# One-hots of 128 lanes and a masked copy of the gathered rows, in a GNN kernel's collecting stages

## The chip, the cores and the metric

The kernel runs on one core of a Trainium2 chip. The metric is the device time of one execution in microseconds; the time before is the median of three runs.

## The reference

There are 12500 nodes with 16 features, and 400000 edges (src, dst), sorted by dst. Two layers, each followed by a residual and a layernorm over the 16 features:

```python
# layer 0
F_s = householder(reflection(xs, xd)); F_d = householder(reflection(xd, xs))
L_sd = -einsum('eki,ekj->eij', F_s, F_d)
msg_s = coef[:, None] * einsum('eij,ej->ei', L_sd, xd)
msg_d = coef[:, None] * einsum('eji,ej->ei', L_sd, xs)
out = relu(x - zeros.at[src].add(msg_s) - zeros.at[dst].add(msg_d))
# layer 1, twice (W1, b1), (W2, b2): gcn_conv and tanh
agg = segment_sum((h @ W)[row] * norm[:, None], col, num_segments=N)
```

What matters here is the sum over the edges of a node: the scatter to dst in layer 0, and the segment sums of the two graph convolutions. Below they are collect 0, 1 and 2.

## The kernel before

Nodes are kept in blocks of 128 (NB = 98 of them), and two blocks make a wide block of 256 nodes (NW = 49). The kernel sorts the edges twice into wide blocks, by src and by dst, in chunks of CH = 8 edges a partition. Each stage that needs a node's row for an edge, or adds an edge's row to a node, does it with one-hot matrices on TensorE: a tile is 128 edges (one a partition), its one-hot says which of the block's nodes the edge belongs to. Values are split into three bf16 pieces, so a row has 3 * D = 48 columns.

Around the change there are these stages, in the profiled execution's time. The message stage (2416 to 5083 us) computes the messages in src order, adds those for src, and writes those for dst to DRAM rows of CH * RW values (msg_rows); RW = 3 * D + 2 leaves room for the key of the edge's dst node behind the 48 values. Collect 0 (5083 to 5803) gathers these rows in dst order and adds them to the nodes. Then, twice, a stage that expands the nodes' values in src order and writes them to val_rows (5847 to 6340, 6993 to 7488), and a stage that collects them in dst order (6340 to 6962, 7488 to 8105).

A collect has G2 = 293 groups of 16 tiles, one after the other, all in loops written out for each engine, four groups a pass (q = 0 to 3):

- GpSimd (gather_rows, the gather at L601) issues one indirect DMA a group into got[q]. It waits until TensorE is done with the group four before, and in collect 0 for that group's keys too.
- ScalarE in collect 0 (copy_keys, L913 and L914) copies the keys from the rows to dst_key, in pairs; collects 1 and 2 use them again. In all three (far_hots2) it makes the one-hots of the last 2 tiles by Abs and Relu (L895, L901, L906).
- VectorE (collect, turn) waits in collect 0 for the keys, then adds the sums of the group three before (add_group: L1812 loads an address, L1679 adds 96 columns from PSUM to acc), then makes the one-hots of the other 14 tiles (lanes, L1670) in lane_hot2[q]. A one-hot is 256 wide, both halves of a wide block.
- TensorE (sums, L1159) waits for rows, one-hots and a free PSUM bank, and runs for each tile one matmul for the lower and one for the upper 128 nodes, each with 48 columns.

acc holds 48 columns for each block of 128 nodes, lower then upper. Behind a collect VectorE reduces the three pieces to agg (L1850, L1884) and goes on with the node-wise part. src_rel, dst_rel and later dst_key share the memory of rel_all. The names lane_hotb and wide_hotb in the profile are the buffers 0, 1 and 2, 3 of lane_hot2; wide_hotb is also used by the expanding stages.

## Time and profile before

| | us |
|---|---|
| median of 3 runs (lowest to highest) | 7817.33 (7814.12 to 7823.55) |
| profiled execution, first to last instruction | 8142.6 |
| message stage, in the profile | 2667 |
| collect 0, 1, 2 | 720, 622, 617 |
| the two expanding stages | 493, 495 |

The profiled execution stands for its kernel with one time only, its span; nothing is given of what lies around that, and it is 325 us longer than the median. Times in a timeline count from the span's start. In its rows a number in brackets is the idle time of the engine before the instruction, and what ended it; "issue" means that the profile shows nothing that the engine waited for. An instruction's next one can start up to 0.1 us before the shown end. Rows of TensorE merge a run of matmuls (x32).

### The profile page before, as it was taken

The numbers are of one execution on the slowest core, as the hardware profiler recorded it, in microseconds if no ns is written. First come the engines' busy times: TensorE is split into PE (matmuls) and PEld (weight loads), VectorE is DVE, ScalarE is ACT, GpSimd is POOL, SyncE is SP. The second block draws the span as 40 slices with busy tenths as digits, with TensorE's granted clock in tenths as the row PEclk, the third lists the DMA queues.
The fourth block names the chain that finished last, engine by engine and source line by source line (L and its number), as shares of the span: only waits on it lengthen the run. The fifth ranks groups of instructions, "written<-read, shape, count | busy, mean of one in ns | idle before, by whom it ended". The sixth has DMA issues, their size and how long they took to land.

```text
span 8142.6 us, 284433 instructions
## 1 busy us (share of the span) xinstructions
PE 5258.0 (65%) x105060; PEld 4635.4 (57%) x105060; DVE 7026.3 (86%) x9716; ACT 5313.1 (65%) x12774; POOL 3318.7 (41%) x2217
## 2 busy tenths in 40 slices
PE   3431000677759899999999987566466666566665
PEld 2321000566647777777777776555455566555665
DVE  6559993555559999999999999999899999999999
ACT  4534130222228888888888887888666788567886
POOL 3340006666643333333333332555200788101886
PEclk8655555888878777778777777555566555566555
DMA  3000000888863333333333332333499433697333
GB/s 45 12 20 5 0 13 13 307 292 299 294 225 99 105 105 103 104 103 104 104 105 105 105 104 84 94 85 85 112 295 296 123 94 94 199 295 237 94 94 78
DMA packets 510651, 1043.86 MB, mean 128 GB/s; under 512 B 125636, under 2 KB 316420, under 8 KB 497508
## 3 DMA queue, kind: packets, MB, share of 16 engines
q1 hardware_dynamic: 376804, 761.05, 27.3%
q0 software_dynamic: 113856, 281.66, 13.7%
q10 hardware_dynamic: 19904, 0.13, 0.2%
q8 instruction: 38, 0.62, 0.0%
q14 instruction: 49, 0.40, 0.0%
HBM read 756.40 MB, written 286.18 MB: 128 GB/s over the span
## 4 chain that ended last, share of the span: by engine, by line
DVE 32%; issue 25%; PE 21%; ACT 7%; DVEq 6%; another core or an unknown queue 3%; ACTq 2%; POOL 2%; DMA 2%; POOLq 0%; SPq 0%
PE ps L1159 11%; PE ps L1054 6%; DVE wide_hotb L1871 3%; PE ps L1193 3%; DVE keys L1387 3%; DVEq L1812 3%; ACT apartb L901 3%; DVEq L1674 2%; DVE whole L1763 2%; DVE mirr L1767 2%; DVE acc L1679 2%; DVE low L1770 2%; DVE prod L1731 2%; DVE keys L1386 2%
## 5 line engine op out<-in xcount | busy, mean ns | idle before, releaser
L601 POOL DMA_INDIRECT xs_buf<-xd_rows,src_idx x488 | 871.2, 1785 | 1809.0 <-DVE mirr L1767 1668.3
L601 POOL DMA_INDIRECT got<-val_rows,dst_idx x586 | 1045.4, 1784 | 1259.6 <-DMA val_rows<-val_out 1075.3
L1871 DVE TENSOR_SCALAR wide_hotb<-sw_inb,slot_id 128x2048 bf16<-128x2048 bf16 x976 | 922.1, 1015 | 53.0 <-PE ps L1193 52.9
L1133 PEld LDWEIGHTS ps<-w2c,hid 128*128 128x128 f32 x7808 | 942.8, 197 | 13.4
L1084 PEld LDWEIGHTS ps<-wide_tab,wide_hot 128*128 128x128 bf16 x23424 | 634.1, 102 | 521.7 <-DVE wide_hot L1664 493.7
L1133 PE MATMUL ps<-w2c,hid 128*128 128x32 f32 x7808 | 919.8, 278 | 0.0
L1670 DVE TENSOR_TENSOR lane_hotb<-rel_all,iota_b 128x3584 bf16<-128x3584 bf16 x441 | 892.8, 2025 | 11.5 <-ACT rel_all L914 7.0
L1670 DVE TENSOR_TENSOR wide_hotb<-rel_all,iota_b 128x3584 bf16<-128x3584 bf16 x438 | 886.8, 2025 | 0.2 <-ACT rel_all L914 0.2
L1159 PE MATMUL ps<-got,lane_hotb 128*128 128x48 bf16 x14112 | 642.2, 215 | 369.3 <-DVE acc L1679 187.4
L1193 PE MATMUL ps<-wide_tabb,wide_hotb 128*128 128x48 bf16 x15616 | 626.3, 205 | 369.2 <-DVE wide_hotb L1871 253.4
L1054 PE MATMUL ps<-row_tab,dst_hot 128*128 128x64 bf16 x15744 | 669.9, 204 | 273.2 <-issue 238.3
L1159 PE MATMUL ps<-got,wide_hotb 128*128 128x48 bf16 x14016 | 635.2, 214 | 321.5 <-DVE acc L1679 187.3
L1159 PEld LDWEIGHTS ps<-got,lane_hotb 128*128 128x128 bf16 x14112 | 585.6, 117 | 425.9 <-DVE acc L1679 224.4
L901 ACT ACTIVATE apartb<-iota_b,rel_negb 128x256 bf16<-128x256 bf16 x1758 | 797.6, 500 | 40.1 <-ACT rel_negb L895 0.3
L1193 PEld LDWEIGHTS ps<-wide_tabb,wide_hotb 128*128 128x128 bf16 x15616 | 580.7, 111 | 414.9 <-ACT val_out L952 341.3
L1084 PE MATMUL ps<-wide_tab,wide_hot 128*128 128x32 bf16 x23424 | 659.8, 185 | 226.0 <-DVE wide_hot L1664 222.6
L1159 PEld LDWEIGHTS ps<-got,wide_hotb 128*128 128x128 bf16 x14016 | 582.4, 117 | 374.2 <-issue 186.5
L1054 PEld LDWEIGHTS ps<-row_tab,dst_hot 128*128 128x128 bf16 x15744 | 586.8, 105 | 356.7 <-issue 333.6
L601 POOL DMA_INDIRECT src_key<-chunk_keys,src_idx x488 | 609.7, 1249 | 338.6 <-ACT xd_out L758 197.1
L758 ACT ACTIVATE xd_out<-ps 128x512 f32<-128x512 f32 (+1 forms) x384 | 199.8, 534 | 618.2 <-remote 402.9
L1617 DVE COPY_PREDICATED xd_out<-row_upper,ps 128x512 f32<-128x512 uint8 (+1 forms) x384 | 217.4, 636 | 415.2 <-ACT xd_out L758 403.4
L601 POOL DMA_INDIRECT got<-msg_rows,dst_idx x293 | 408.2, 1393 | 353.6 <-ACT rel_all L914 269.5
(392 smaller groups left out, 11976.3 us busy)
## 6 DMA issues: line engine op xcount, KB each, us to landing
dw_in<-dst_wide SPq DMA_DIRECT2D x96, 1312.0 KB
xd_rows<-xd_out SPq DMA_DIRECT2D x128, 984.0 KB
sw_in<-src_wide SPq DMA_DIRECT2D x244, 512.0 KB, 4.3
sw_inb<-src_wide SPq DMA_DIRECT2D x244, 512.0 KB, 5.1
val_rows<-val_out SPq DMA_DIRECT2D x488, 192.0 KB, 4.1
sw_inb<-src_byte SPq DMA_DIRECT2D x244, 256.0 KB
msg_rows<-msg_out SPq DMA_DIRECT2D x244, 200.0 KB, 2.4
dw_in<-dst_byte SPq DMA_DIRECT2D x32, 656.0 KB
```

Of the source, the lines that this page charges most:

```text
L601: return pool.indirect_dma_start(out=into, out_offset=None, in_=table, in_offset=bass.IndirectOffsetOnAxis(index, 0))
L901: last = act.activation(apart2[:, t, :], iota_b[:, :], ACT.Abs, bias=rel_neg2[:, t:t + 1])
L1054: last = mm(ps_unit[(3 * k + n) % 4][:, t - c, :, :], dst_hot[k % 2][:, t * P:(t + 1) * P], tab[:, part, :, :], start=part == 0, stop=part ...
L1084: last = mm(ps_x[:, h, t, :], wide_hot[s][:, half, e:e + P], wide_tab[s][:, h, at:at + 2 * D], start=half == part == 0, stop=half == 1 and ...
L1133: last = mm(ps_v[:, h * CH + t, :], hid[:, t % 4, at:at + P], w2c[:, :], start=False, stop=h == 1 and t == CH - 1)
L1159: last = mm(ps_sum[q][:, half * 3 * D:(half + 1) * 3 * D], lane_hot2[q][:, t, half * P:(half + 1) * P], got[q][:, at:at + 3 * D], start=t ...
L1193: last = mm(ps_val[s * 2 + h][:, t, :], wide_hot2[s][:, half, e:e + P], wide_tab2[s][:, h, half * 3 * D:(half + 1) * 3 * D], start=half == ...
L1387: return v.tensor_tensor(to_hi, lo, hi, ALU.max)
L1617: last = v.copy_predicated(xd_out[k % 4][:, c:d, 0:2 * D], row_upper[k % 4][:, c:d].unsqueeze(2).to_broadcast([P, d - c, 2 * D]), ps_unit[ ...
L1670: return v.tensor_tensor(to.rearrange("p t (j k) -> p t j k", k=2), rel.unsqueeze(2).to_broadcast(shape), iota_b[:, :].rearrange("p (j k) ...
L1812: at = dve.value_load(wide_at[0:1, 2, bass.ds(i * 4 + q, 1)], min_val=0, max_val=NW * 6 * D)
L1871: last = v.tensor_scalar(wide_hot2[q % 2][:, half, :], sw_in2[q][:, :], slot_id[:, half:half + 1], None, ALU.is_equal)
```

## The change

In the collects a one-hot is 128 lanes wide: the lane is the dst node modulo 128, whichever half of the wide block it is in. Each row buffer got[q] has a second plane. VectorE multiplies the gathered values by a mask that is 1 where the edge's node is in the upper half and 0 elsewhere, and writes the product to the second plane. One matmul a tile takes both planes, 96 columns: its sums are those of all edges of a lane, and those of the upper ones. acc so holds "both halves" and "upper"; the lower half is their difference, taken once behind each collect (join_halves). Since collect 0 adds to an acc that the message stage has filled by lower and upper, one addition ahead of it turns lower into both.

The mask comes from the key: dst_rel is split into lane and half (dst_part), both go into the two spare places of a message row, and ScalarE copies the half to dst_half in collect 0. In collects 1 and 2 VectorE now waits for the gathered rows itself, between its one-hots and the product. The one-hots of all four buffers lie in wide_hot2. ScalarE's one-hots are 128 wide too.

```diff
-        rel_all = sb("rel_all", [P, 4 * G2 * CH], BF16)
-        src_rel = rel_all[:, 0:LW * CH]
-        dst_rel = rel_all[:, LW * CH:2 * LW * CH]
-        dst_key = rel_all[:, :].rearrange("p (n k) -> p n k", k=2)
+        src_rel = sb("src_rel", [P, LW * CH], BF16, of=pr)
+        dst_part = sb("dst_part", [P, LW * CH, 2], BF16, of=pr)
...
-        got = [sb(f"got{k}", [P, 2 * CH * RW], BF16, of=pf) for k in range(4)]
-        lane_hot2 = [sb(f"lane_hotb{k}", [P, 2 * CH, 2 * P], BF16, of=pf) for k in range(2)]
+        got = [sb(f"got{k}", [P, 2, 2 * CH * RW], BF16, of=pf) for k in range(4)]
+        dst_key = sb("dst_key", [P, 2 * CH * G2, 2], BF16, of=pf)
+        dst_half = sb("dst_half", [P, 2 * CH * G2, 2], BF16, of=pf)
-        apart2 = sb("apartb", [P, max(FAR_TILES2), 2 * P], BF16, of=pf)
+        apart2 = sb("apartb", [P, max(FAR_TILES2), P], BF16, of=pf)
-        lane_hot2 += [of[:, :, :].rearrange("p h (t c) -> p (h t) c", c=2 * P) for of in wide_hot2]
+        lane_hot2 = [wide_hot2[k % 2][:, k // 2, :].rearrange("p (t c) -> p t c", c=P) for k in range(4)]
-        rest_t = sb("rest_t", [P, NB, D], of=pf)
+        rest_t = tmp
...
-                act.activation(msg_out[s][:, 0, :, 3 * D], dst_rel[:, bass.ds(i * (8 * CH) + 2 * CH * q, 2 * CH)], ACT.Copy)
+                act.activation(msg_out[s][:, 0, :, 3 * D:RW], dst_part[:, bass.ds(i * (8 * CH) + 2 * CH * q, 2 * CH), :], ACT.Copy)
...
-                    last = act.activation(apart2[:, t, :], iota_b[:, :], ACT.Abs, bias=rel_neg2[:, t:t + 1])
+                    last = act.activation(apart2[:, t, :], iota_b[:, 0:P], ACT.Abs, bias=rel_neg2[:, t:t + 1])
...
+                act.activation(dst_half[:, bass.ds(i * (8 * CH) + 2 * CH * q, 2 * CH), :], half, ACT.Copy)
...
+            act.wait_ge(p3_done, 1)
             for q in range(4):
                 keys_turn(0, q)
...
-                        for half in range(2):
-                            last = mm(ps_sum[q][:, half * 3 * D:(half + 1) * 3 * D], lane_hot2[q][:, t, half * P:(half + 1) * P],
-                                      got[q][:, at:at + 3 * D], start=t == half == 0, stop=t == 2 * CH - 1 and half == 1)
+                        last = mm(ps_sum[q].rearrange("p (k c) -> p k c", k=2), lane_hot2[q][:, t, :],
+                                  got[q][:, :, at:at + 3 * D], start=t == 0, stop=t == 2 * CH - 1)
...
-            v.tensor_tensor(dst_rel[:, 0:n], dst_rel[:, 0:n], missing[:, :], ALU.add).then_inc(rel_ready, 1)
+            step(v.tensor_tensor(dst_rel[:, 0:n], dst_rel[:, 0:n], missing[:, :], ALU.add))
+            step(v.tensor_scalar(dst_part[:, 0:n, 1], dst_rel[:, 0:n], float(P), None, ALU.is_ge))
+            v.scalar_tensor_tensor(dst_part[:, 0:n, 0], dst_part[:, 0:n, 1], -float(P), dst_rel[:, 0:n], ALU.mult, ALU.add).then_inc(rel_ready, 1)
...
+                    width = RW if l == 0 else 3 * D
+                    whole_row, upper_row = (got[q % 4][:, k, 0:2 * CH * width].rearrange("p (t c) -> p t c", c=width)[:, :, 0:3 * D]
+                                            .rearrange("p t (j k) -> p t j k", k=2) for k in range(2))
+                    half = dst_half[:, bass.ds(i * (8 * CH) + 2 * CH * q, 2 * CH), :].unsqueeze(2).to_broadcast([P, 2 * CH, 3 * D // 2, 2])
...
-                    lanes(lane_hot2[q % 4][:, 0:near, :], rel, near).then_inc(lhot2_ready[l], 1)
+                    lanes(lane_hot2[q % 4][:, 0:near, :], rel, near, P)
+                    if l > 0:
+                        seen = l * (G2 // 4 + (q % 4 == 0))
+                        dve.wait_ge(rows_got[q % 4], i * 16 + (XD_GOT + seen * 16 + 16))
+                    v.tensor_tensor(upper_row, whole_row, half, ALU.mult).then_inc(lhot2_ready[l], 1)
...
+            def join_halves():
+                step(v.tensor_reduce(agg[:, :, :], acc_v, AX.X, ALU.add))
+                step(v.tensor_tensor(agg_halves[:, :, 0, :], agg_halves[:, :, 0, :], agg_halves[:, :, 1, :], ALU.subtract))
+
+            step(v.tensor_tensor(acc_halves[:, :, 0, :], acc_halves[:, :, 0, :], acc_halves[:, :, 1, :], ALU.add))
             collect(0)
...
-            step(v.tensor_reduce(agg[:, :, :], acc_v, AX.X, ALU.add))
+            join_halves()
```

## Rows read from the trace of the kernel before

**Rows 1.** The page's first line: the profiled execution.
```profile
span 8142.6 us, 284433 instructions
```

**Rows 2.** Stretches of the three collects: busy time by engine, clock, DMA.
```profile
core 0: us, PE busy (x) PEld busy (x) DVE busy (x) ACT busy (x) POOL busy (x), PEclk, DMA share, GB/s
5083.00:5803.00 720.00, 427.41 (x9376) 389.73 (x9376) 641.70 (x585) 630.55 (x1758) 408.20 (x293) 0.50 0.33 88
6340.00:6962.00 622.00, 423.81 (x9376) 388.07 (x9376) 612.86 (x585) 503.33 (x1166) 522.65 (x293) 0.51 0.35 97
7488.00:8105.00 617.00, 425.79 (x9376) 390.02 (x9376) 610.43 (x584) 499.71 (x1161) 520.74 (x292) 0.50 0.34 94
```

**Rows 3.** Timeline of collect 1, three groups: start, us, engine, line, operation.
```profile
6597.26 1.79 POOL L601 DMA_INDIRECT got<-val_rows,dst_idx  x1 [0.30 <-issue]
...
6600.24 0.26 DVE L1679 TENSOR_TENSOR acc<-acc,ps 128x96 f32 x1
6600.41 2.03 DVE L1670 TENSOR_TENSOR wide_hotb<-rel_all,iota_b 128x3584 bf16<-128x3584 bf16 x1
...
6600.56 1.46 PE L1159 MATMUL ps<-got,lane_hotb 128*128 128x48 bf16 x32 [0.64 <-DVE acc L1679]
...
6601.46 1.79 POOL L601 DMA_INDIRECT got<-val_rows,dst_idx  x1 [0.31 <-issue]
...
6602.34 0.26 DVE L1679 TENSOR_TENSOR acc<-acc,ps 128x96 f32 x1
```

**Rows 4.** Timeline of GpSimd in the gathers of the sort's keys.
```profile
591.51 0.94 POOL L601 DMA_INDIRECT keys<-key_rows,seg_idx  x1 [0.30 <-issue]
```

**Rows 5.** Timeline of collect 0, two groups.
```profile
5601.08 1.38 POOL L601 DMA_INDIRECT got<-msg_rows,dst_idx  x1 [1.04 <-ACT rel_all L914]
...
5601.71 1.46 PE L1159 MATMUL ps<-got,wide_hotb 128*128 128x48 bf16 x32 [0.90 <-DVE wide_hotb L1670]
...
5602.11 2.02 DVE L1670 TENSOR_TENSOR lane_hotb<-rel_all,iota_b 128x3584 bf16<-128x3584 bf16 x1
...
5602.94 0.20 ACT L913 ACTIVATE rel_all<-got 128x16 bf16 x1
5603.05 0.29 ACT L914 ACTIVATE rel_all<-got,alone 128x16 bf16 x1
5603.44 1.50 POOL L601 DMA_INDIRECT got<-msg_rows,dst_idx  x1 [0.98 <-ACT rel_all L914]
...
5603.71 0.91 ACT L901 ACTIVATE apartb<-iota_b,rel_negb 128x256 bf16<-128x256 bf16 x2
...
5604.27 1.34 PE L1159 MATMUL ps<-got,lane_hotb 128*128 128x48 bf16 x29 [1.10 <-DVE lane_hotb L1670]
5604.29 0.25 DVE L1679 TENSOR_TENSOR acc<-acc,ps 128x96 f32 x1 [0.16 <-issue]
...
5604.73 0.72 ACT L906 ACTIVATE lane_hotb<-apartb,ones 128x512 bf16<-128x512 bf16 x1
5605.35 0.20 ACT L913 ACTIVATE rel_all<-got 128x16 bf16 x1
```

**Rows 6.** Timeline of the message stage, beside a gather.
```profile
3605.35 2.36 POOL L601 DMA_INDIRECT xs_buf<-xd_rows,src_idx  x1 [6.70 <-DVE mirr L1767]
3605.60 0.68 DVE L1670 TENSOR_TENSOR lane_hot<-rel_st,iota_b 128x1024 bf16<-128x1024 bf16 x1
...
3606.20 0.68 DVE L1775 TENSOR_TENSOR msg_out<-low 128x512 bf16<-128x512 f32 x1
```

**Rows 7.** Timeline behind collect 2.
```profile
8110.74 1.79 DVE L1885 TENSOR_TENSOR agg<-agg,node_t 128x1568 f32<-128x1568 f32 x1
```

**Rows 8.** DMA view, 6598 to 6602: rate in slices of 0.1 us.
```profile
GB/s 92 323 215 369 62 123 0 0 0 0 0 0 0 0 0 0 0 184 230 230 276 46 184 384 246 123 62 0 0 0 0 0 0 0 0 0 0 0 276 138
```

**Rows 9.** Chain of waits near the end of collect 0: start, us, what.
```profile
5702.41 4.03 DMA got<-msg_rows,dst_idx
```

**Rows 10.** Timeline of VectorE ahead of the message stage.
```profile
2417.24 0.72 DVE L1779 MEMSET msg_out<- 128x800 uint32 x1 [12.01 <-DMA src_byte<-turned]
```

More of the change, by code:

```diff
@@ L127, in gnn_kernel @@
         row_at = sb("row_at", [1, P], I32)
-        wide_at = sb("wide_at", [1, 4, LW], I32)
+        wide_at = sb("wide_at", [1, 3, LW], I32)
         wide_base = sb("wide_base", [P, LW])
         alone = sb("alone", [P, LW])
-        upper = sb("upper", [P, COLS, P], U8)
         b2_parts = sb("b2_parts", [P, 3, 2 * D], BF16)
@@ L134, in gnn_kernel @@
         b2_one = sb("b2_one", [P, 2 * D], BF16)
+        pu = ExitStack()
+        ctx.enter_context(pu)
+        upper = sb("upper", [P, COLS, P], U8, of=pu)
         po = ExitStack()
@@ L249, in gnn_kernel @@
         pc.close()
+        pu.close()
         acc = sb("acc", [P, (NB + 2) * 3 * D])
-        rel_all = sb("rel_all", [P, 4 * G2 * CH], BF16)
-        src_rel = rel_all[:, 0:LW * CH]
-        dst_rel = rel_all[:, LW * CH:2 * LW * CH]
-        dst_key = rel_all[:, :].rearrange("p (n k) -> p n k", k=2)
+        pr = ExitStack()
+        ctx.enter_context(pr)
+        src_rel = sb("src_rel", [P, LW * CH], BF16, of=pr)
+        dst_part = sb("dst_part", [P, LW * CH, 2], BF16, of=pr)
         pd = ExitStack()
@@ L265, in gnn_kernel @@
         missing = sb("missing", [P, NST * CH], BF16, of=pd)
+        dst_rel = sb("dst_rel", [P, NST * CH], BF16, of=pd)
         pd.close()
@@ L653, in gather_rows @@
                             pool.wait_ge(key_copied, g - 3)
-                    gather(got[g % 4][:, 0:2 * CH * width], pairs, dst_idx[:, g:g + 1]).then_inc(rows_got[g % 4], 16)
+                    gather(got[g % 4][:, 0, 0:2 * CH * width], pairs, dst_idx[:, g:g + 1]).then_inc(rows_got[g % 4], 16)
             pool.wait_ge(p3_done, 1)
@@ L910, in copy_keys @@
                 act.wait_ge(rows_got[q], i * 16 + (XD_GOT + 16))
-                rel = got[q][:, :].rearrange("p (t c) -> p t c", c=RW)[:, :, 3 * D].unsqueeze(2).to_broadcast([P, 2 * CH, 2])
+                keys_of = got[q][:, 0, :].rearrange("p (t c) -> p t c", c=RW)
+                rel, half = (keys_of[:, :, c].unsqueeze(2).to_broadcast([P, 2 * CH, 2]) for c in (3 * D, 3 * D + 1))
                 to = dst_key[:, bass.ds(i * (8 * CH) + 2 * CH * q, 2 * CH), :]
+                act.activation(dst_half[:, bass.ds(i * (8 * CH) + 2 * CH * q, 2 * CH), :], half, ACT.Copy)
                 act.activation(to[:, 0:CH, :], rel[:, 0:CH, :], ACT.Copy)
@@ L1666, in wide_hot_half, with lanes @@
                     ins.then_inc(whot_ready, 1)
-            def lanes(to, rel, n):
-                shape = [P, n, P, 2]
+            def lanes(to, rel, n, w):
+                shape = [P, n, w // 2, 2]
                 return v.tensor_tensor(to.rearrange("p t (j k) -> p t j k", k=2), rel.unsqueeze(2).to_broadcast(shape),
-                                       iota_b[:, :].rearrange("p (j k) -> p j k", k=2).unsqueeze(1).to_broadcast(shape), ALU.is_equal)
+                                       iota_b[:, 0:w].rearrange("p (j k) -> p j k", k=2).unsqueeze(1).to_broadcast(shape), ALU.is_equal)
             def acc_at(i, q, h, kind):
@@ L1689, in lane_hots @@
                         dve.wait_ge(pacc_ready, i * 4 + (q - 1))
-                last = lanes(lane_hot[s][:, at, :], rel_st[s][:, at, :], at.stop - at.start)
+                last = lanes(lane_hot[s][:, at, :], rel_st[s][:, at, :], at.stop - at.start, 2 * P)
                 if at.stop == NEAR:
@@ L1883, in _ @@
                 collect(l)
-                step(v.tensor_reduce(agg[:, :, :], acc_v, AX.X, ALU.add))
+                join_halves()
                 step(v.tensor_tensor(agg[:, :, :], agg[:, :, :], node_t[:, :, :], ALU.add))
```

3 lines of the change are left out of this document (added).

## Prediction

> **What bounds the kernel now.** The change touches the three stages that collect (layer 0, 1 and 2), so I read the profile by stretches first [rows 1, 2]. The profiled execution spans 8142.6 us and the timed runs have a median of 7817, 325 us less. I work the sum out as a difference in the trace and take it off the median. The stretches show collect 0 in 720 us and collects 1 and 2 in 622 and 617, each with 293 groups. VectorE is busy for 642, 613 and 610 of them, TensorE's matmuls for about 425, and its granted clock stands at 0.50 to 0.51, the 1.2 GHz level.
>
> Next, the timeline of a few groups in each kind of stage. In collect 1 [rows 3] VectorE starts an accumulation (L1679), 0.17 us later the one-hots of the next group (L1670, 2.03), and 1.93 us after those the next accumulation, with no idle time: 2.10 us per group. GpSimd issues a gather just as often (1.79 busy plus 0.30), but it isn't an equal bound. Where VectorE is quiet, a gather takes 0.94 and the next starts 1.25 us later [rows 4]. The gather of 6601.46 ends at 6603.25, 0.81 us after the one-hots beside it (6600.41 + 2.03 = 6602.44): it waits for them, so its period is VectorE's and not one of its own.
>
> In collect 0 [rows 5] the period is 2.41 us (ACT L913, 5602.94 to 5605.35), and it is ScalarE's: L913 0.11, L914 and L895 with their waits 0.66, two L901 and a wait 1.02, L906 0.62, then the next. VectorE has gaps there: the key is copied at 5603.34, and the accumulation starts only at 5604.29, 0.95 us of its sequencer's work later.
>
> **The change, part by part.**
>
> *One-hots of 128 lanes.* 14 tiles × 128 = 1792 elements for 3584. From 1024 elements in 0.68 and 3584 in 2.03 [rows 3, 6] the slope is 0.527 ns an element: 1792 cost 1.09, and 1.01 until the next instruction may start.
>
> *The masked copy.* 16 tiles × 48 = 768 bf16 elements. It reads and writes in pairs, with one operand repeated, as the one-hots do, so I take their slope: 0.55, spacing 0.47. Lower bound: that slope. Upper bound: the fp32 rate of one element a tick, 512 in 0.68 [rows 6] and 1568 in 1.79 [rows 7], which gives 0.95, spacing 0.87. I take 0.55, since the access pattern is nearest to L1670's.
>
> *VectorE's turn* is then 0.17 + 1.01 + 0.47 = 1.65 us in place of 2.10.
>
> *TensorE.* 16 matmuls of 96 columns instead of 32 of 48: 1536 columns either way. The group of 32 takes 1.46, 46 ns each, near the 40 ns of 48 columns at 1.2 GHz, so weight loads are already hidden and I leave it at 1.46 (bounds: 0.73, half of it, at the 2.4 GHz level, and 1.46). ScalarE: L901 and L906 halve. From L901's 256 columns (two spaced 0.41 take 0.91, so 0.50 each) and L906's 512 (0.72) the slope is 0.86 ns [rows 5]: 2 × 128 columns less in L901 are 0.22, 256 less in L906 another 0.22. One more copy (dst_half) costs 0.12 by L913's spacing. Collect 0's ScalarE period: 2.41 − 0.44 + 0.12 = 2.09.
>
> *The new wait.* In collects 1 and 2 VectorE's queue now waits for the gathered rows before the multiply. Behind it stand the next accumulation, its address load and the next one-hots, and TensorE and the gather after them. So the four row buffers make a loop. From the end of a multiply: TensorE 0.15 later (one-hots to matmuls, 5604.13 to 5604.27), 1.46 of matmuls, gather start 0.27 later (5603.17 to 5603.44): 1.88. The gather: 0.94 free, more if VectorE holds it. Landing: the gather that ended at 6599.05 moves its bytes in the slices from 6599.7 to 6600.7 [rows 3, 8]; with its completion I use 1.75 after the end. The upper end comes from [rows 9], where start to landing is 4.03. After landing the sequencer issues the multiply (0.2, an estimate from its address steps) and then needs the 0.95 to the next accumulation; with 0.17 + 1.01 + 0.55 the next multiply ends 2.88 after landing. Unhindered, 5 turns = 1.88 + 0.94 + 1.75 + 2.88 = 7.45, 1.49 a turn, below 1.65. But one-hots and multiply now run back to back. A gather that began at 3605.35 beside three such two-input instructions ended at 3607.71, 0.83 after the last of them (3606.20 + 0.68) [rows 6], so it gets its turn only behind the multiply. Then the landing is 2 turns + 0.82 + 1.75 after the multiply, and 5T = 2T + 5.45, T = 1.82; at 1.82 the gather's start falls into the gap behind the multiply again and it isn't held. The turn must lie between 1.65 and 1.82; I take 1.72.
>
> By the Trainium skill (SBUF — State Buffer, section Who interferes with whom) a VectorE instruction with two SBUF inputs shuts out a GpSimd instruction that reads SBUF for its whole length, if it came first. By this rule, the trace agrees: 0.83 after the third of three. It speaks against this change, which puts a second such instruction right behind the first; with every gather held by it the turn is 1.82 and the gain in the two stages 164 us, with none held it is 1.65 and 264 us.
>
> Collects 1 and 2: 586 × (2.10 − 1.72) = 223 us.
>
> *Collect 0.* The loop there: 0.27 + 1.35 (two gathers of [rows 5] took 1.38 and 1.50, and the gap on VectorE grows) + 1.75 + 0.1 + 0.52 (copies) + 0.95 + 0.17 + 1.01 + 0.55 + 0.15 + 1.46 = 8.28, 2.07 a turn. Where a gather takes 4.03 from its start to landing, as the chain of waits shows near the stage's end [rows 9], 0.93 more: 2.30. ScalarE wants 2.09. I take 2.14: 293 × (2.41 − 2.14) = 79 us.
>
> *The rest.* One fp32 addition over 2352 elements once (2.6) and three over 784 (0.97 each), from 1568 in 1.79: 5.5, all on the path. The two extra steps that split dst_rel (3904 elements each: by the two slopes 2.1 to 4.1) lie beside the turned source lists: VectorE idles 12.01 us there before L1779 [rows 10]; without that cover they would cost up to 8. The wider key field in the message rows adds 16 elements to a ScalarE copy, 0.01 × 244, beside VectorE: nothing, 3 us at most. rest_t on tmp's memory adds no wait, both being VectorE's own. The one-hots now all lie in wide_hot2, free once the matmuls of the stage before are done, which VectorE already waits for.
>
> Sum: 223 + 79 − 6 = 296. 7817 − 296 = 7521.
>
> **The rivals.**
>
> 1. *The multiply runs at one element a tick.* In layer 0 its rows start every 100 bytes, and one operand is a pair repeated, which speaks for it a little; L1670, with the same repeated pair, speaks against. Turn: 0.17 + 1.01 + 0.87 = 2.05, 29 us in collects 1 and 2, and some 65 in collect 0: 7817 − 29 − 65 + 6 = 7729.
>
> 2. *The buffer loop becomes the bound:* gathers land as late as the 4.03 row, or are held through two turns. 5T = 7.45 + 0.95 unhindered is 1.68, held 2.13; halfway, 1.91, plus 0.2 for collect 0 at 2.21: 586 × 0.19 + 293 × 0.20 − 6 = 164, so 7653. For it: the two-input instructions back to back. Against it: the landing of [rows 3, 8] is 3.4 us after its gather's start though VectorE held that gather too, and a turn longer than about 1.8 opens the gap behind the multiply.
>
> 3. *Slower: the multiply costs more than it frees.* The place is VectorE's turn in collects 1 and 2, the price the multiply's spacing, the point 2.10 − 1.18 = 0.92. At half of the fp32 rate (1.7) the turn is 2.88, + 457 us there and about + 150 in collect 0: 8400. No row shows such a rate for a contiguous run.
>
> 4. *Better than forecast:* if the gathers stay out of the way, 1.65 in both late collects (264) and 2.07 in collect 0 (100): 7817 − 358 = 7459. If TensorE's clock rose with its denser work, its 1.46 would shrink to 0.73, which gives the loop 0.15 a turn and could bring this about.
>
> **How the numbers follow.** Forecast with rival 4 as its good end: 0.74 (its own range 7440 to 7600). Rival 2: 0.10. Rival 1: 0.09. Slower: 0.04. No change, where gains are undone by new holds on the gather (2.10 again): 0.03. The range from 7430 to 7690 leaves out rival 1, the slower case and the no change, and takes in rival 2. A difference under 0.2% (16 us) is about what a measurement can't tell from none. Faster 0.93, same 0.03, slower 0.04.
>
> **What would show it.** The one-hots at 1.09; the multiply at 0.55 or 0.95; VectorE's period in collects 1 and 2 between 1.65 and 1.82, with short idle times before the accumulation; gathers whose lengths vary between 0.94 and 1.8; collect 0 with ScalarE gap-free at 2.1; PE groups still 1.3 to 1.5. A multiply above 0.95, idle time on VectorE charged to the gather's DMA, or gathers longer than a turn would make the forecast wrong.

## The result and the profile after

The changed kernel takes 7520.5 us (median of 4, 7512.72 to 7544.89) against 7815.73 for the kernel before beside it (4 runs): a ratio of 0.9628, 95% interval 0.9616 to 0.964. The prediction said 7521.

The stretches of the three collects come first; they stand against [rows 2]. Each runs from the first gather's start to the last one's, and so leaves out the last few microseconds that the windows of [rows 2] hold. Taken the same way in the trace of before, the three are 710, 614 and 612 us.

```profile
span 7512.3 us, 258924 instructions
```

```profile
core 0: us, PE busy (x) PEld busy (x) DVE busy (x) ACT busy (x) POOL busy (x), PEclk, DMA share, GB/s
4753.00:5390.00 637.00, 415.93 (x4624) 356.44 (x4624) 502.12 (x868) 543.24 (x2034) 324.29 (x293) 0.52 0.37 99
5937.00:6445.00 508.00, 285.85 (x4628) 241.99 (x4629) 478.92 (x868) 376.37 (x1163) 347.54 (x293) 0.87 0.43 118
6976.00:7467.00 491.00, 262.88 (x4624) 221.62 (x4624) 476.69 (x867) 377.23 (x1165) 333.23 (x293) 0.94 0.44 117
```

The collects lost 73, 106 and 121 us, 300 together. VectorE is now busy for 479 of 508 and 477 of 491 us, and is still the busiest engine of collects 1 and 2. Two columns were not expected: TensorE's granted clock is 0.87 and 0.94 instead of 0.50, and its matmuls are busy for 286 and 263 us instead of about 425, for as many columns.

The profile's groups give VectorE's new instructions their price:

```profile
L1680 DVE TENSOR_TENSOR wide_hotb<-dst_key,iota_b 128x1792 bf16<-128x1792 bf16 x879 | 951.3, 1082 | 13.6 <-ACT dst_key L922 9.1
L1839 DVE TENSOR_TENSOR got<-got,dst_half 128x768 bf16<-128x768 bf16 x879 | 483.0, 549 | 20.2 <-DMA got<-val_rows,dst_idx 19.8
```

One-hots 1.08 us, multiply 0.549 us: both as the slope from [rows 3, 6] gave them. By the Trainium skill (VectorE: DVE Perf Modes, What auto-detection actually checks) a tensor_tensor runs at two elements a tick if all its tensors are 16-bit with steps of one, and no faster. The trace agrees, though one operand is a repeated pair: from 768 elements in 0.549 us and 1792 in 1.082 it is 0.52 ns an element, half of the 1.05 that the fp32 rows give (512 in 0.68 [rows 6], 1568 in 1.79 [rows 7]).

Two stretches of the timeline answer to [rows 3]. A turn is the time from one group to the next. First collect 2 where the granted clock is 1.00:

```profile
7201.06 1.08 DVE L1680 TENSOR_TENSOR wide_hotb<-dst_key,iota_b 128x1792 bf16<-128x1792 bf16 x1
...
7201.20 0.91 PE L1167 MATMUL ps<-got,wide_hotb 128*128 128x96 bf16 x16 [0.78 <-DVE acc L1689]
7202.06 0.55 DVE L1839 TENSOR_TENSOR got<-got,dst_half 128x768 bf16<-128x768 bf16 x1
...
7202.38 1.05 POOL L607 DMA_INDIRECT got<-val_rows,dst_idx  x1 [0.58 <-PE ps L1167]
7202.53 0.24 DVE L1689 TENSOR_TENSOR acc<-acc,ps 128x96 f32 x1
...
7202.69 1.08 DVE L1680 TENSOR_TENSOR wide_hotb<-dst_key,iota_b 128x1792 bf16<-128x1792 bf16 x1
```

From one-hots to one-hots it is 1.63 us with no idle time. Then the end of collect 1, where the clock is 0.70:

```profile
6330.00 0.25 DVE L1689 TENSOR_TENSOR acc<-acc,ps 128x96 f32 x1 [0.85 <-issue]
6330.17 1.08 DVE L1680 TENSOR_TENSOR wide_hotb<-dst_key,iota_b 128x1792 bf16<-128x1792 bf16 x1
...
6331.95 1.46 PE L1167 MATMUL ps<-got,wide_hotb 128*128 128x96 bf16 x16 [1.72 <-DVE acc L1689]
...
6335.08 1.08 DVE L1680 TENSOR_TENSOR wide_hotb<-dst_key,iota_b 128x1792 bf16<-128x1792 bf16 x1
...
6335.65 1.33 POOL L607 DMA_INDIRECT got<-val_rows,dst_idx  x1 [0.30 <-issue]
6336.08 0.55 DVE L1839 TENSOR_TENSOR got<-got,dst_half 128x768 bf16<-128x768 bf16 x1
```

Some turns have a gap on VectorE ahead of the addition (0.85, the sequencer's address work when it was stopped at the rows), the group of matmuls takes 1.46, and over 25 us the turn averages 1.80 to 1.83. So collects 1 and 2 have two regimes, stretches of 1.64 us a turn and stretches of about 1.8, the fast and the slow regime below. Windows show when:

```profile
5944.00:6100.00 156.00, 81.72 (x1476) 68.93 (x1476) 151.53 (x277) 118.63 (x367) 104.61 (x91) 0.96 0.42 122
6100.00:6300.00 200.00, 108.91 (x1904) 91.76 (x1902) 195.22 (x355) 153.47 (x474) 139.03 (x120) 0.94 0.41 116
6300.00:6448.00 148.00, 97.79 (x1281) 83.51 (x1281) 135.16 (x244) 102.83 (x314) 101.94 (x80) 0.70 0.43 107
```

With 91, 120 and 80 gathers the turn is 1.71, 1.67 and 1.85 us.

The regimes differ in what a gather meets. In the fast stretches it starts beside the multiply, 0.27 behind a group of matmuls, and ends 0.82 behind the multiply (7202.38 + 1.05 = 7203.43, the multiply ends at 7202.61). Where the mean turn over eight groups is under 1.66, 325 of 331 gathers do. Where it is over 1.75 the kinds alternate: of 156 gathers 64 end 0.82 behind the one-hots, 53 behind the multiply, and 39 aren't held.

The change from one regime to the other can be seen too:

```profile
6096.08 1.11 POOL L607 DMA_INDIRECT got<-val_rows,dst_idx  x1 [0.53 <-PE ps L1167]
...
6099.24 1.22 POOL L607 DMA_INDIRECT got<-val_rows,dst_idx  x1 [2.05 <-PE ps L1167]
...
6102.62 0.56 DVE L1839 TENSOR_TENSOR got<-got,dst_half 128x768 bf16<-128x768 bf16 x1 [0.18 <-DMA got<-val_rows,dst_idx]
...
6103.57 0.25 DVE L1689 TENSOR_TENSOR acc<-acc,ps 128x96 f32 x1 [0.39 <-issue]
...
6105.53 0.90 PE L1167 MATMUL ps<-got,wide_hotb 128*128 128x96 bf16 x16 [1.28 <-DVE got L1839]
...
6107.73 1.46 PE L1167 MATMUL ps<-got,wide_hotb 128*128 128x96 bf16 x16 [1.30 <-DVE acc L1689]
```

Until 6096.08 a gather starts every 1.64 us. The next one comes 3.16 us later, 1.5 late (the profile charges the wait to TensorE, whose group had ended at 6097.45). VectorE is stopped at the rows, two turns take 2.38 and 2.21 us, and only then does a group of matmuls take 1.46 us instead of 0.85. Counted from 0, this is group 94 of collect 1. Group 204 and groups 21, 131 and 241 of collect 2 are late in the same way, each 110 gathers behind the last; a slow stretch follows four of the five. In the kernel before the same five gathers start 0.3 late, and VectorE, which doesn't wait for rows there, keeps its 2.10.

Collect 0, against [rows 5]:

```profile
5101.73 0.22 ACT L920 ACTIVATE dst_half<-got 128x32 bf16 x1
...
5103.14 0.26 DVE L1689 TENSOR_TENSOR acc<-acc,ps 128x96 f32 x1 [0.40 <-issue]
...
5103.36 0.51 ACT L912 ACTIVATE wide_hotb<-apartb,ones 128x256 bf16<-128x256 bf16 x1
5103.77 0.24 ACT L920 ACTIVATE dst_half<-got 128x32 bf16 x1
```

ScalarE's row runs without a gap, 2.04 us from one copy of the halves to the next; VectorE waits 0.40 ahead of its addition.

Behind the collects the additions cost what the prediction took:

```profile
4752.85 2.61 DVE L1873 TENSOR_TENSOR acc<-acc 128x2352 f32<-128x2352 f32 x1 [0.18 <-DVE acc L1689]
```

```profile
5404.91 0.98 DVE L1871 TENSOR_TENSOR agg<-agg 128x784 f32<-128x784 f32 x1
```

### The profile page after: what moved, and what is told of

The parts are those of the page before. It is cut to its first block, busy times and chain, and to the rows that moved or that the text cites. A ratio compares the mean times of both kernels' runs of the same rounds, so it can differ in the third digit from the quotient of the medians.

```text
span 7512.3 us, 258924 instructions
## 1 busy us (share of the span) xinstructions
PE 4798.4 (64%) x90996; PEld 4205.3 (56%) x90996; DVE 6624.4 (88%) x10601; ACT 4958.7 (66%) x13067; POOL 2921.5 (39%) x2217
## 4 chain that ended last, share of the span: by engine, by line
DVE 34%; issue 25%; DMA 13%; ACT 7%; PE 7%; DVEq 6%; POOL 6%; ACTq 2%; POOLq 0%; SPq 0%
DMA xd_rows<-xd_out 7%; DVE wide_hotb L1897 4%; DMA got<-val_rows,dst_idx 3%; PE ps L1201 3%; DVE keys L1395 3%; DVEq L1684 3%; POOL found L607 2%; DVE whole L1773 2%; DVE mirr L1777 2%; DVE low L1780 2%; DVE prod L1741 2%; DVE acc L1689 2%; DVE keys L1394 2%; DVEq L1822 2%; PE ps L1167 2%
## 5 line engine op out<-in xcount | busy, mean ns | idle before, releaser
L1167 PE MATMUL ps<-got,wide_hotb 128*128 128x96 bf16 x14064 | 978.1, 237 | 686.5 <-DVE acc L1689 375.1
L607 POOL DMA_INDIRECT got<-val_rows,dst_idx x586 | 683.3, 1166 | 1393.8 <-DMA val_rows<-val_out 1076.0
L1680 DVE TENSOR_TENSOR wide_hotb<-dst_key,iota_b 128x1792 bf16<-128x1792 bf16 x879 | 951.3, 1082 | 13.6 <-ACT dst_key L922 9.1
L907 ACT ACTIVATE apartb<-iota_b,rel_negb 128x128 bf16<-128x128 bf16 x1758 | 609.7, 394 | 39.8
L912 ACT ACTIVATE wide_hotb<-apartb,ones 128x256 bf16<-128x256 bf16 x879 | 446.3, 508 | 241.9 <-PE ps L1167 211.1
L866 ACT ACTIVATE hid<-ps,b1c 128x1024 f32<-128x1024 f32 x488 | 517.0, 1118 | 4.1 <-PE ps L1127 4.1
L1689 DVE TENSOR_TENSOR acc<-acc,ps 128x96 f32 x1367 | 340.2, 249 | 202.6 <-issue 177.8
L951 ACT ACTIVATE wide_tabb<-parts 128x96 bf16 x976 | 276.0, 283 | 359.4 <-issue 280.7
L1839 DVE TENSOR_TENSOR got<-got,dst_half 128x768 bf16<-128x768 bf16 x879 | 483.0, 549 | 20.2 <-DMA got<-val_rows,dst_idx 19.8
L1680 DVE TENSOR_TENSOR lane_hot<-rel_st,iota_b 128x1024 bf16<-128x1024 bf16 x732 | 498.1, 680 | 0.0
```

Of the source, the lines that this page charges most:

```text
L607: return pool.indirect_dma_start(out=into, out_offset=None, in_=table, in_offset=bass.IndirectOffsetOnAxis(index, 0))
L866: act.activation(hid[:, :, at], ps[:, 0:4 * BANK].rearrange("p (b c) -> p b c", b=4)[:, :, at], ACT.Relu, bias=b1c[:, :]).then_inc(hid_rea ...
L907: last = act.activation(apart2[:, t, :], iota_b[:, 0:P], ACT.Abs, bias=rel_neg2[:, t:t + 1])
L1167: last = mm(ps_sum[q].rearrange("p (k c) -> p k c", k=2), lane_hot2[q][:, t, :], got[q][:, :, at:at + 3 * D], start=t == 0, stop=t == 2 * ...
L1680: return v.tensor_tensor(to.rearrange("p t (j k) -> p t j k", k=2), rel.unsqueeze(2).to_broadcast(shape), iota_b[:, 0:w].rearrange("p (j k ...
L1689: v.tensor_tensor(to, to, of, ALU.add).then_inc(added, 1)
```

## The experiments

Each kernel's time stands beside runs of the kernel before from its own series of measurements. In the series of the kernel before once more, of the one without the multiply and of the first with two matmuls, the kernel before takes 8136 us, as in its first profile (8142.6); in the others it takes 7810 to 7820. The excess lies ahead of the collects.

### The kernel before, once more

No edit. 

> The kernel before, profiled once more, nothing changed. The first profile of it spans 8142.6 us, the timed runs have a median of 7816. If that profile was disturbed only ahead of the collects (collect 0 begins at 5083 us there and at 4753 in the changed kernel's profile), this one spans about 7815, its collects last 720, 622 and 617 us again, within 1%, and the granted clock in them is 0.50 again. If the low clock in the collects belonged to that one execution, the clock in collects 1 and 2 is well above 0.50 here and the collects are no longer than before.

Measured: 8126.03, and 711, 615 and 612 us for the collects at clock 0.50 to 0.52. It spans 8124.3 us and not about 7815, but the excess lies ahead of the collects, which repeat to 1 us. One of the longer stages there, the gathers of src_key, took 900 and 897 us in the two traces of before and 802 in the trace of after. So the 325 us of which the prediction only said that the profile was longer don't belong to the collects, and taking the sum as a difference was sound. What makes the difference stays open: 8136 and 7810 were both measured on chip number 4.

### Without the multiply

The first four groups keep it.

```diff
-                    lanes(lane_hot2[q % 4][:, 0:near, :], rel, near, P)
+                    last = lanes(lane_hot2[q % 4][:, 0:near, :], rel, near, P)
...
-                    v.tensor_tensor(upper_row, whole_row, half, ALU.mult).then_inc(lhot2_ready[l], 1)
+                    if first_four:
+                        v.tensor_tensor(upper_row, whole_row, half, ALU.mult).then_inc(lhot2_ready[l], 1)
```

> Leaves out the masked multiply in all groups but the first four of each collect, so the upper halves' sums are wrong; the wait for the rows stays in VectorE's queue. Theory (VectorE's turn sets collects 1 and 2): the turn falls from 1.64 by the multiply's spacing 0.47 to 1.17, unless the buffer loop stops it: with TensorE at 2.4 GHz 0.15 + 0.80 + 0.27 + 0.94 + 1.76 + about 2.3 from landing to the one-hots' end = 6.2 over 5 turns = 1.25. So 1.25 to 1.35 in collects 1 and 2 (1.74 and 1.68 before), and collect 0 by about 0.1 a group, ScalarE-bound at 2.05: 7520 - 240 - 20 = 7260. Rival (the loop of row buffers sets the turn already): the turn falls by the multiply's share of the loop only, 0.55 / 5 = 0.11, 65 us in both collects: about 7440.

Measured: 7836.03 beside 8135.66, ratio 0.9638 (0.9612 to 0.9663): no better than the changed kernel's 0.9628. The stretches:

```profile
6224.00:6733.00 509.00, 314.45 (x4624) 273.54 (x4624) 363.13 (x580) 376.24 (x1162) 386.87 (x292) 0.79 0.45 118
7265.00:7758.00 493.00, 310.76 (x4629) 269.78 (x4630) 361.39 (x581) 376.18 (x1161) 364.93 (x293) 0.80 0.45 116
```

VectorE is busy for 363 us instead of 479, and the stretch is as long: 115 us of work taken away turned into waits. The chain of waits over 7500 to 7510 says which:

```profile
by line: DMA got<-val_rows,dst_idx 30.9%; DVE wide_hotb L1680 19.3%; DVEq L1822 16.7%; issue 16.3%; POOL got L607 13.9%; PE ps L1167 8.7%; DVE acc L1689 3.1%; DVEq L1689 1.6%; DVEq L1847 1.2%; DVEq L1680 0.8%; DVEq L1687 0.4%; DVEq L1821 0.
```

It goes round the four row buffers: landing, VectorE's sequencer (L1822, the address of the addition), one-hots, gather. Both expectations fell: mine had this loop at 1.25 us a turn, its rival had it shrink with the multiply, and the turns stayed at 1.74 and 1.69. The wait for the rows with what is queued behind it is a second bound, at about 1.7 us a turn, right beside VectorE's 1.65.

### The multiply twice

The first copy goes to a spare buffer.

```diff
+                    v.tensor_tensor(spare[q % 4][:, 0:2 * CH * width].rearrange("p (t c) -> p t c", c=width)[:, :, 0:3 * D]
+                                    .rearrange("p t (j k) -> p t j k", k=2), whole_row, half, ALU.mult)
```

> The multiply is issued twice in every group, the first into a spare buffer. Leaving the multiply out changed the collects by under 1% (turns of 1.74 and 1.69), so two limits lie close together: VectorE's own work, 1.64, and the loop of row buffers. Theory (both are limits, the larger one counts): doubled, VectorE's work is 1.64 + 0.47 = 2.11 a group, the larger by far: 586 times 0.40 = 235 us in collects 1 and 2, and 0.47 / 4 = 0.12 a group in collect 0, 35 us: 270 above the changed kernel beside it. Rival (only the loop counts): 0.47 / 5 a group, 55 us, and 35: 90 above. The granted clock: if a turn of 2.1 us keeps it down, it is near 0.5 in collects 1 and 2.

Measured: 7781.96 beside 7809.87, ratio 0.9965 (0.9953 to 0.9978), 261 us above the changed kernel in the same series, where the theory said 270.

```profile
5966.00:6588.00 622.00, 418.09 (x4624) 359.75 (x4624) 608.68 (x1156) 376.29 (x1162) 293.41 (x292) 0.51 0.35 97
7120.00:7731.00 611.00, 414.62 (x4624) 356.70 (x4624) 607.94 (x1154) 375.95 (x1161) 487.30 (x292) 0.51 0.34 94
```

So VectorE's work is a limit too: 0.47 us more of it put the turn at 2.10, as VectorE's own work has it, and the granted clock is back at 0.51. TensorE's columns are those of the changed kernel, in the same 16 matmuls. So a longer turn by itself brought the clock down.

### Two matmuls a tile

```diff
-                        last = mm(ps_sum[q].rearrange("p (k c) -> p k c", k=2), lane_hot2[q][:, t, :],
-                                  got[q][:, :, at:at + 3 * D], start=t == 0, stop=t == 2 * CH - 1)
+                        for k in range(2):
+                            last = mm(ps_sum[q][:, k * 3 * D:(k + 1) * 3 * D], lane_hot2[q][:, t, :],
+                                      got[q][:, k, at:at + 3 * D], start=t == k == 0, stop=t == 2 * CH - 1 and k == 1)
```

> Only the joined matmul is undone: two matmuls of 48 columns for each tile, with the same one-hot loaded twice, on the masked copy. VectorE's and ScalarE's work is that of the changed kernel. Theory (the one matmul a tile is worth nothing in itself, since 1536 columns stream either way): TensorE's group stays at 0.8 at the high level of the clock or 1.46 at the low one, time within 0.3% of 7520. Rival (the joined matmul is what brought the clock up from 0.50 to 0.95): the clock falls to about 0.5 in collects 1 and 2, TensorE's group takes 1.46, the loop sets the turn at 1.75 to 1.82, and 586 times 0.08 to 0.15 us come on top: 7565 to 7610.

Measured: 7902.47 beside 8135.66, ratio 0.972 (0.9695 to 0.9745). The interval of the changed kernel, from another series, lies below it. It was run again where the kernel before takes 7816 us:

> The run with two matmuls of 48 columns a tile once more, since it ran on the other chip (kernel before 8136 us) and the changed kernel didn't run beside it there. Its collects 1 and 2 had turns of 1.84 and 1.82 with a granted clock of 0.73 and 0.72 against 1.74 and 1.68 at 0.87 and 0.94 in the changed kernel on this kind of chip. Theory (more weight loads keep TensorE's clock down, and the low clock puts the gather's start behind the gap after the multiply, so turns are 1.8 and not 1.64): 35 to 60 us above the changed kernel's 7521. Rival (the chip was the difference): within 15 us of 7521.

Measured: 7552.92 beside 7815.66, ratio 0.9662 (0.9645 to 0.9678), 32 us above the changed kernel (7520.5 and 7520.59 in two other series, whose intervals lie below this one), just short of the theory's 35, with clocks of 0.79 and 0.72:

```profile
5930.00:6451.00 521.00, 338.98 (x9280) 307.90 (x9280) 482.07 (x868) 377.83 (x1165) 351.57 (x293) 0.79 0.43 115
6983.00:7508.00 525.00, 356.88 (x9248) 324.70 (x9248) 486.38 (x867) 376.40 (x1163) 415.37 (x293) 0.72 0.41 109
```

The prediction gave the joined matmul nothing. It is worth some 30 us, all of it in collects 1 and 2, where more of the time passes in the slow regime. Collect 0 is unmoved (638).

### The changed kernel, once more

> The changed kernel itself, as the reference for the runs beside it, since the kernel before took 8136 us on the chip of the first experiments and 7816 on that of the result. Its collects are 637, 508 and 491 us in its first profile. If the two chips differ only ahead of the collects, it is 295 to 315 us below the kernel before here too, and its collects are within 2% of those. If the low clock costs more on this chip, collects 1 and 2 are longer (turns of 1.75 to 1.82) and it gains less, 200 to 260.

Measured: 7520.59 beside 7809.87, ratio 0.9616 (0.9596 to 0.9635); collects 637, 508 and 507. That is 289 us below, just short of the expected 295, and collect 2 is 3% longer than in the first profile. How long each collect stays in the fast regime differs between executions (collect 2: clock 0.86 and 507 us here, 0.94 and 491 above).

### One-hots of the next group ahead of the wait

In collects 1 and 2 VectorE makes the one-hots of group g + 1 before it waits for the rows of g.

```diff
+                        if ahead:
+                            hots_of(i, q + 1)
+                        seen = l * (G2 // 4 + (q % 4 == 0))
+                        dve.wait_ge(rows_got[q % 4], i * 16 + (XD_GOT + seen * 16 + 16))
```

> In collects 1 and 2 VectorE makes the one-hots of the next group before it waits for this group's rows, so only the multiply stands behind the wait; the work is the same. Theory (the sequencer's 0.95 us and the one-hots between the rows' landing and the next multiply make the loop as long as VectorE's work): the loop becomes 4 turns = 0.15 + 0.8 to 1.46 + 0.27 + 0.94 + 1.76 + 0.75 = 4.7 to 5.3, 1.2 to 1.33 a turn, VectorE's 1.64 alone counts, and the turns fall from 1.74 and 1.68 to 1.65: 25 + 10 = 35 us less than the changed kernel beside it, more if its turns are longer on this chip. Rival (the excess over 1.64 comes from single late gathers, whatever the order): within 10 us.

Measured: 7536.9 beside 7809.87, ratio 0.9653 (0.9637 to 0.9669). No gain: the collects were 498 and 500 in the profiled execution, and the timed runs were 16 us above the changed kernel, where the theory had 35 below and its rival 10 either way. Taking the one-hots out of what follows the wait was not enough. The rival's reason, single late gathers, fits the trace better: here too those of groups 94 and 204 of collect 1 come 3.16 us behind the one before, and longer turns follow.

### The addition first in collect 0

```diff
                     if l == 0:
-                        dve.wait_ge(key_copied, i * 4 + (q + 1))
...
+                    if l == 0:
+                        dve.wait_ge(key_copied, i * 4 + (q + 1))
```

> In collect 0 VectorE adds the sums of the group three before ahead of its wait for the keys, instead of behind it; nothing else. Theory (ScalarE's 2.05 us a group sets collect 0): the median turn stays at 2.05, only the excess of the mean, 2.18, can shrink: at most 0.1 a group, 30 us. Rival (the loop through key, address load, addition, one-hots, multiply and matmuls sets it): the 0.95 us of sequencer work leave a loop of four turns, 0.24 a group at the most, down to ScalarE's 2.05 or, if that isn't a limit, 1.9: 40 to 80 us.

Measured: 7521.93 beside 7809.87, ratio 0.9617 (0.9597 to 0.9637). Collect 0 fell by 14 us to 623, the whole not measurably. With the addition out of the way, collect 0's mean turn is 2.13, near ScalarE's own 2.05, and the gain is within the theory's 30 us.

### One-hots ahead and no multiply

The one-hots of the next group ahead of the wait, and the multiply left out.

> Both suspected limits of collects 1 and 2 are taken away at once: no multiply (all groups but the first four; the upper halves' sums are wrong), and the one-hots of the next group are made ahead of the wait for the rows. Without the multiply alone the turn stayed at 1.69 to 1.74, with the one-hots ahead alone at 1.71. Theory (VectorE's work 1.64 and a loop of row buffers with VectorE's sequencer in it of 1.7 lie side by side): now VectorE has 1.17 and the loop 4 turns = 0.8 to 1.46 + 0.27 + 0.94 + 1.76 + 0.1, about 1.0 to 1.15, so the next limits are ScalarE's 1.43 and GpSimd's 1.25 plus holds: turns of 1.43 to 1.5, 125 to 165 us below the changed kernel: 7355 to 7395, with 20 less for collect 0. Rival (GpSimd, held by the one-hots, sets a turn of 1.6 to 1.7 whatever VectorE does): within 40 us of the changed kernel.

Measured: 7423.84 beside 7815.66, ratio 0.9495 (0.9462 to 0.9528), between the theory and its rival. The collects took 458 and 468 us. Averaged over 25 us their turn is mostly either near 1.38 or near 1.75, as two of its windows show:

```profile
5945.00:6060.00 115.00, 69.61 (x1314) 58.40 (x1315) 100.31 (x166) 103.56 (x321) 89.92 (x83) 1.00 0.51 141
...
7250.00:7300.00 50.00, 24.68 (x466) 20.67 (x464) 36.38 (x59) 37.70 (x117) 41.38 (x29) 1.00 0.41 114
```

That is 1.39 (83 gathers in 115 us) and 1.72 (29 in 50), both at a granted clock of 1.00. So a slower regime exists where VectorE has only 1.2 us of work; the multiply isn't its cause, and a low clock isn't needed for it.

### A gap between one-hots and multiply

```diff
+                    v.memset(gap[:, 2 * (q % 4):2 * (q % 4) + 2], 0.0)
```

> One memset of two numbers a partition is put between the one-hots and the multiply, in all three collects; it has no SBUF input. Theory (a gather waits for the end of an unbroken run of VectorE instructions with two SBUF inputs, and this is what makes turns of 1.8 when TensorE's clock is low): the memset costs 0.08 to 0.1 a group, but opens a second place for the gather; gathers take 0.95 to 1.1 in the median, no stretch of collects 1 and 2 has turns above 1.78, all are near 1.72 to 1.74: within 0.3% of the changed kernel. Rival (the gather's hold has no part in the long turns): the stretches of 1.8 become 1.9, and the kernel is 50 to 60 us slower.

Measured: 7530.75 beside 7815.66, ratio 0.9649 (0.9625 to 0.9672). The stretches of 1.64 a turn went to 1.65, those of 1.80 stayed there. The time is within the theory's 0.3%, but its way there fell, since stretches of 1.80 remain, and the rival's 1.9 fell too. How far the memset parted the two instructions isn't shown: the multiply still starts 1.01 us behind the one-hots, 1.00 before, and gathers in fast stretches still take 1.12. What is shown is that none of the 586 gathers of collects 1 and 2 was held through both instructions here, 6 were in the changed kernel, and the slow regime is as slow without them. Its chain over 7200 to 7250:

```profile
by line: POOL got L608 87.4%; issue 17.1%
...
7199.22 1.68 POOL got L608
7200.90 0.30 issue
7201.20 1.61 POOL got L608
7202.82 0.30 issue
7203.12 1.34 POOL got L608
```

In the slow regime GpSimd issues gathers one behind the other, each held for a different time; 262 of the 293 gathers of this collect end 0.82 behind the one-hots.

### Collect 0: less for ScalarE; collects 1 and 2: one-hots ahead

```diff
-    FAR_TILES, FAR_TILES2 = 4, (2, 2, 2)
+    FAR_TILES, FAR_TILES2 = 4, (1, 2, 2)
```

With it the two edits above, the addition first in collect 0 and the one-hots ahead in the others.

> A version that could beat both kernels: in collect 0 the addition ahead of the wait for keys and one tile instead of two made by ScalarE; in collects 1 and 2 the one-hots ahead. Theory for collect 0 (ScalarE's 2.05 and the loop lie side by side, since the addition ahead alone left the turn at 2.13): ScalarE falls to 1.65, VectorE's own is 1.71, the loop 7.2 / 4 = 1.8 to 1.85: collect 0 takes 545 instead of 637 us, and the kernel 7430 to 7450. Rival (only the loop counts in collect 0, TensorE's low clock and late gathers in it): the turn stays above 2.0 and the kernel above 7490.

Measured: 7455.66 beside 7815.66, ratio 0.9536 (0.952 to 0.9552), 6 us above the theory's 7450.

```profile
4742.00:5307.00 565.00, 355.72 (x4624) 302.30 (x4624) 513.59 (x868) 440.70 (x1741) 326.66 (x292) 0.68 0.42 111
5855.00:6365.00 510.00, 294.41 (x4632) 249.78 (x4633) 482.30 (x868) 376.61 (x1163) 349.31 (x293) 0.85 0.44 118
6894.00:7419.00 525.00, 325.43 (x4624) 276.93 (x4624) 485.52 (x865) 376.56 (x1163) 413.87 (x293) 0.76 0.41 109
```

Collect 0 went from 637 to 565 us, 20 more than the theory's 545. Alone the addition gave 14 of the 72; the rest came with a tile moved from ScalarE (441 us busy, from 543) to VectorE (514, from 502). With the addition ahead, ScalarE was therefore collect 0's bound, and its row without a gap says the same of the change as it was made. Collects 1 and 2 gained nothing, as before.

### The address read ahead too

In collects 1 and 2 the turn is rotated: load the address of the addition, wait for the rows, multiply, add, one-hots.

```diff
+                    if warm:
+                        at = dve.value_load(wide_at[0:1, 2, bass.ds(i * 4 + (q - 3), 1)], min_val=0, max_val=NW * 6 * D)
+                    seen = l * (G2 // 4 + ((q - 1) % 4 == 0))
+                    dve.wait_ge(rows_got[(q - 1) % 4], i * 16 + (XD_GOT + seen * 16 + (16 * ((q - 1) // 4) + 16)))
+                    masked(i, q - 1)
+                    if warm:
+                        dve.wait_ge(pacc2_ready[l], i * 4 + (q - 2))
+                        add_at(i * 4 + (q - 3), at, ps_sum[(q - 3) % 4], acc2_added[l])
+                    if ahead:
+                        hots_of(i, q + 1)
```

> The kernel of e9_both (collect 0 with the addition first and one tile for ScalarE; collects 1 and 2 with the one-hots ahead), and in collects 1 and 2 the address of the accumulation is also read ahead of the wait for the rows, which takes some 0.6 of the 0.95 us that VectorE's sequencer spends on them out of the loop from the landed rows to the next released gather. Theory that this loop, over about five turns, holds the slow stretches at 1.80 us a turn: they shrink by 0.6 / 5 = 0.12 us, the stretches at 1.65 stay where VectorE's own work puts them, collects 1 and 2 come to about 490 us each and the kernel to 7400 to 7430 us. Rival, that GpSimd's held gathers, issued back to back, hold the slow stretches whatever the sequencer does: within 15 us of e9_both (7456 us).

Measured: 7419.76 (7414.24 to 7425.35) beside 7819.85, ratio 0.9489 (0.9473 to 0.9505). This is the fastest kernel here, 400 us below the kernel before and 101 below the change as it was made.

```profile
5854.00:6348.00 494.00, 261.44 (x4626) 220.25 (x4627) 478.72 (x868) 376.61 (x1163) 397.00 (x292) 0.94 0.44 122
6884.00:7372.00 488.00, 264.17 (x4624) 222.66 (x4624) 477.16 (x867) 376.58 (x1163) 396.86 (x292) 0.94 0.43 117
...
5860.00:6270.00 410.00, 216.41 (x3952) 182.12 (x3952) 406.34 (x742) 318.93 (x985) 328.17 (x246) 0.97 0.43 122
6270.00:6348.00 78.00, 45.03 (x674) 38.13 (x675) 72.38 (x128) 54.55 (x169) 65.08 (x43) 0.80 0.44 106
```

Up to 6270 VectorE is busy for 406 of 410 us; only the last 78 us are slower, at 1.81 a turn (43 gathers), and collect 2 ends the same way. The rival fell by 36 us against its 15. The theory's total (7400 to 7430) and its 490 us a collect held, but not its way there: it had slow stretches at 1.68, and there are none but the end, which stayed as slow as it was. The timeline shows how the steady turn looks:

```profile
6008.36 0.55 DVE L1834 TENSOR_TENSOR got<-got,dst_half 128x768 bf16<-128x768 bf16 x1
...
6008.99 1.08 DVE L1680 TENSOR_TENSOR wide_hotb<-dst_key,iota_b 128x1792 bf16<-128x1792 bf16 x1
...
6009.56 1.33 POOL L607 DMA_INDIRECT got<-val_rows,dst_idx  x1 [0.30 <-issue]
...
6011.20 1.33 POOL L607 DMA_INDIRECT got<-val_rows,dst_idx  x1 [0.30 <-issue]
```

The gather of 6009.56 starts beside the one-hots (6008.99 + 1.08 = 6010.07) and ends 0.82 behind them, and so do 281 and 280 of the 293 gathers in the two collects. It is the long instruction that holds them here, as in the slow regime of the changed kernel, and the turn is 1.64 all the same. So what a gather meets doesn't make a turn slow. The difference is in the waits. In the changed kernel's fast stretches a gather waits for TensorE first (0.58 at 7202.38). Here it follows the one before by 0.30 and waits for nothing, its buffer being free already: the loop has room to spare. The five late gathers show it too. They start 2.21 to 2.26 us behind the one before and not 3.16, and a slow stretch follows only the last, group 241, which begins collect 2's slow end. Two things changed at once, the address load and the order of the turn; the run doesn't tell their shares apart.

## Why the prediction was right

**The sum.** Forecast: 79 us for collect 0, 223 for collects 1 and 2, less 6. Measured in the traces: 73, and 106 + 121 = 227; the added steps behind the collects 2.61 and three of 0.98, as forecast. The two that split dst_rel took 2.35 and 4.65 us, 7.0 where the upper end was 8.2 (the second of them runs at 1.2 ns an element), and VectorE still idled for 4.88 us behind them, so they stayed covered. The collects give 300, less 5.5 the 295 that the medians show.

**VectorE's turn and the multiply's rate** were right: 1.64 for 1.65, 0.549 for 0.55. Rival 1 (0.95) is gone by that row, rival 3 too. Doubling the multiply shows that the turn counts in full.

**The new wait** was right as a bound and wrong as a picture. The prediction had 1.65 and 1.82 as ends and took 1.72 between them as an even mean. The trace has two regimes near those ends, one after the other: 1.64 at a granted clock of 1.00, and 1.80 to 1.83 where the clock goes up and down. The mean over both collects came out at 1.71. That owes something to luck, since it depends on how long each regime lasts. The hit of the upper end, 1.82, owes still more to luck. The formula 5T = 2T + 5.45 has every gather held behind the multiply, and in the slow stretches 53 of 156 are. For those behind the one-hots, which end 0.47 earlier, it gives 5T = 2T + 4.98, or 1.66, so that its agreement with the measured 1.80 is no proof of its picture.

**The step that failed** is "so weight loads are already hidden and I leave it at 1.46", and with it the sign "PE groups still 1.3 to 1.5": in the fast regime a group takes 0.85. Only rival 4 named a rise of the clock, "with its denser work". The doubled multiply shows that it goes with the turn: 0.51 at 2.10 us, 1.00 at 1.64, with the same matmuls. And two matmuls for one (at 1.64 a turn 0.98 a group instead of 0.85) cost 32 us where the prediction had nothing. The rise moved the total little, since one regime's turn lies 0.08 below the 1.72 that was taken and the other's 0.08 above.

**The hold on the gather.** "It gets its turn only behind the multiply" is true of a gather that starts beside the multiply, and of few others. At 7204.56 a gather of 2.14 went through one-hots and multiply, one of 6 among 586. In the rows of the slow regime above, the gather of 6335.65 ended at 6336.98, 0.82 behind the one-hots (6335.08 + 1.08), with the multiply starting in between. By the Trainium skill (SBUF — State Buffer, Who interferes with whom) the one that issues first keeps the other out for its whole length. The trace agrees for gathers kept out by VectorE: every gather of collects 1 and 2 that was held (over 1.0 us) ends 0.82 behind a two-input instruction. The other way round no run shows a hold: one-hots that start beside a running gather take 1.08 like the others (those of 7400.84 beside the gather of 7400.77). Why a second instruction right behind the first holds the gather on in six cases stays open.

**Collect 0.** 2.06 a turn as a median and 2.18 as a mean, for 2.14. ScalarE's 2.09 was right, and the run that takes a tile from it shows it to be the bound. The prediction's loop, at 2.07, isn't tested by that run, since the addition no longer stands in it.

**Open.** In the changed kernel's two traces every slow stretch but those near a collect's start begins with a late gather. Groups of matmuls still take 0.85 then, so the long turn comes first and the low clock after it. That the lateness is the cause rests on this order in time; no run takes it away, and in the first trace the turns went back to 1.64 at once behind group 21 of collect 2. Open are what makes every 110th gather late, why a slow stretch then lasts for 40 us and more, and why the last kernel still ends both collects at 1.8. Without the multiply a slower stretch also ran at a clock of 1.00, so the clock isn't all of it.

## What to carry to other kernels

Where VectorE is made to wait for data, count what its queue does behind the wait (here an address load and 0.95 us of sequencer time) as part of the buffer loop, and put into the turn's front whatever doesn't need the data. Here the one-hots alone gained nothing there, and with the address load it was 36 us. A wait that is new on the busiest engine also lets in delays that cost nothing before, such as one late gather in 110. When a change shortens the turn of an engine that feeds TensorE, work the sum out at both levels of TensorE's clock, and look at windows of the trace for two regimes before a mean is explained.

## What the runs showed of the hardware

- The granted clock stood at 0.51 with groups of 16 matmuls every 2.1 us and at 1.00 with the same groups every 1.64 us.
- The kernel before takes 7810 to 7820 us in some series and 8136 in one, with the excess ahead of the collects, while the collects repeat closely (612 and 612 us for collect 2).
- Leaving out a quarter of VectorE's work (363 us busy instead of 479) left the collect at 509 us, 508 with it, because a loop of waits lay within 0.1 us of it.
- Every 110th gather of the collects starts late: by 0.3 us in the kernel before, 1.5 in the changed kernel's fast stretches, 0.6 in the last kernel's.
- A gather that VectorE holds ends 0.82 us behind the instruction that held it; one that isn't held takes 0.94.
- A memset of two numbers between two VectorE instructions cost 0.01 us a turn (1.65 for 1.64).
